# Widening 64-row products of a graph network kernel to all 128 rows of TensorE with zeros

## The reference

```python
h = jnp.maximum(_layernorm(x, axis=-1), 0.0)        # [3125, 64], before each layer
# layer 1 (relations): for each of 8 relations r
h_r = x @ W[r]                                       # [N, 64] @ [64, 64]
s, d = h_r @ att_src[r], h_r @ att_dst[r]
out = x @ W_self + b_self + sum over r of the attention sums of h_r
# layer 2 (edge network): [x[start], x[end]] @ We1   = x @ We1[:64] and x @ We1[64:]
# layer 3 (GATv2)
xl, xr = x @ W_l + b_l, x @ W_r + b_r                # [N, 64] @ [64, 256], twice
```

## Time and profile before

| | |
|---|---|
| median of 3 runs | 5458.55 us (5458.1 to 5464.73) |
| the profiled execution | 5454.14 us, span 5452.2 us |
| busy share: PE, DVE, ACT, POOL | 53%, 74%, 14%, 66% |
| mean granted TensorE clock | 0.776 of full speed |
| chain that ended last | POOL 49%, issue 20%, PE 13%, DVE 10%, DMA 5% |

### The profile page before, as it was taken

The page is one execution under the profiler, slowest core; times in us unless marked ns, Lnnn a source line. Parts: engine busy times, 40 slices in busy tenths (PEclk is TensorE's granted clock), DMA queues, the critical chain, the costliest instruction groups (busy, mean ns, idle before and its releaser), DMA issues.

```text
span 5452.2 us, 62157 instructions
## 1 busy us (share of the span) xinstructions
PE 2898.0 (53%) x10645; PEld 1413.7 (26%) x10645; DVE 4041.3 (74%) x10615; ACT 778.0 (14%) x1976; POOL 3590.8 (66%) x3635
## 2 busy tenths in 40 slices
PE   5743374136677000006455555554787777828983
PEld 4522121013566000003122222221333323303332
DVE  8857995245999997655677777745788888888982
ACT  0000021010000014540122222220000000003330
POOL 0677777771777887765777777743777777715651
PEclk9999976565999555555787767765889999869995
DMA  9121364211544338871565555524999999918980
GB/s 382 55 85 37 114 244 153 79 67 66 191 161 163 118 122 316 300 271 49 177 179 181 181 179 181 180 83 150 307 308 310 312 310 306 313 49 313 334 296 13
DMA packets 454207, 1040.84 MB, mean 191 GB/s; under 512 B 129077, under 2 KB 247325, under 8 KB 423796
## 3 DMA queue, kind: packets, MB, share of 16 engines
q1 hardware_dynamic: 162930, 580.42, 29.2%
q0 software_dynamic: 131968, 217.09, 14.5%
q10 hardware_dynamic: 159234, 242.47, 12.7%
HBM read 560.07 MB, written 477.20 MB: 190 GB/s over the span
## 4 chain that ended last, share of the span: by engine, by line
POOL 49%; issue 20%; PE 13%; DVE 10%; DMA 5%; another core or an unknown queue 2%; DVEq 1%; POOLq 0%; ACT 0%; ACTq 0%; SPq 0%
POOL arena L646 32%; POOL weights L679 15%; PE psum L1248 3%; PE psum L1197 3%; PE psum L1198 3%; DMA arena<-tab,ring 3%; PE psum L1032 2%; DVE arena L2029 1%; DVE arena L1770 1%; DVE arena L1534 1%; POOL agg L666 1%; POOL arena L666 1%; DVE arena L1957 1%; DVE arena L1672 0%
## 5 line engine op out<-in xcount | busy, mean ns | idle before, releaser
L646 POOL DMA_INDIRECT arena<-tab,ring x2352 | 2338.1, 994 | 717.5 <-issue 702.8
L1197 PE MATMUL psum<-arena,ident 128*128 128x512 f32 x1176 | 779.5, 751 | 732.4 <-DMA arena<-tab,ring 569.3
L679 POOL DMA_INDIRECT weights<-arena x784 | 829.5, 1058 | 382.9 <-issue 238.7
L1534 DVE SCALAR_TENSOR_TENSOR arena<-arena,ns 128x64 f32<-128x64 f32 (+2 forms) x2351 | 868.6, 369 | 186.6 <-ACT arena L864 49.1
L1198 PE MATMUL psum<-arena,ident 128*128 128x512 f32 x1176 | 724.2, 702 | 0.0
L1197 PEld LDWEIGHTS psum<-arena,ident 128*128 128x128 f32 x1176 | 260.7, 237 | 1155.6 <-issue 627.9
L744 POOL TENSOR_TENSOR arena<-arena,score 128x256 f32<-128x256 f32 x294 | 232.5, 816 | 281.0 <-DMA arena<-spill 126.8
L1248 PE MATMUL psum<-arena,ident 128*128 128x512 f32 x784 | 362.5, 608 | 68.9 <-DVE arena L2029 68.6
L1957 DVE SCALAR_TENSOR_TENSOR arena<-psum,rowb 128x1024 f32<-128x1024 f32 x196 | 239.0, 1219 | 194.8 <-PE psum L1198 194.6
L1198 PEld LDWEIGHTS psum<-arena,ident 128*128 128x128 f32 x1176 | 270.2, 230 | 377.0 <-issue 377.0
L1120 PE MATMUL psum<-arena 64*128 64x400 f32 x512 | 158.6, 705 | 359.9 <-DVE arena L1581 352.2
(11 more groups left out here) (366 smaller groups left out, 4490.0 us busy)
## 6 DMA issues: line engine op xcount, KB each, us to landing
put<-zero SPq DMA_DIRECT2D x98, 1040.0 KB
arena<-put SPq DMA_DIRECT2D x98, 1040.0 KB, 7.7
spill<-arena ACTq DMA_DIRECT2D x98, 1024.0 KB, 5.4
arena<-spill SPq DMA_DIRECT2D x98, 1024.0 KB
state<-arena ACTq DMA_DIRECT2D x147, 512.0 KB, 3.4
weights<-zero SPq DMA_DIRECT2D x1, 51200.0 KB, 130.9
arena<-weights SPq DMA_DIRECT2D x32, 1600.0 KB, 7.8
put<-zero SPq DMA_DIRECT2D x14, 3584.0 KB
```

The lines of the kernel that those rows point to most:

```text
L646: pool.indirect_dma_start(out=rows[:, h, k, :], out_offset=None, in_=table[:, :], in_offset=bass.IndirectOffsetOnAxis(ap=ring[:, h, word + ...
L679: pool.indirect_dma_start(out=weights0[:, :], out_offset=bass.IndirectOffsetOnAxis(ap=words0[:, g, k:k + 1], axis=0), in_=words0f[:, g, K ...
L1197: pe.matmul(place, lhsT=ident[:, :], rhs=rows_of[0][:, s, columns, 0:width], start=True, stop=False)
L1534: beats.add(dve.scalar_tensor_tensor(out=rows[:, s, k, :], in0=before, scalar=mark(ns, g, k), in1=rows[:, s, k, :], op0=ALU.mult, op1=ALU. ...
```

## The change

`hT` and four weight matrices as well as `wa` get all 128 partitions. The kernel goes on writing only partitions 0 to 63 of them. POOL sets partitions 64 to 127 to zero once at the start. `mix` multiplies with the full 128 rows, for the stationary operand and the streaming one, so that the upper half adds products of zeros. PE waits once, ahead of phase 1, until the zeros are there. Everything else, and the products of layer 0 (phase 0), of the edge network's second half (phase 4) and of the feed-forward (phase 6), keeps its 64 rows.

```diff
-        hT = sb("hT", [D, NB, P])
+        hT_full = sb("hT", [P, NB, P])
+        hT = hT_full[0:D, :, :]
...
-        w0_sb, wself_sb, wrel_sb = sb("w0_sb", [D, 2, D]), sb("wself_sb", [D, D]), sb("wrel_sb", [D, R, D])
-        we1_sb = sb("we1_sb", [D, 2, HID])
+        w0_sb, wself_full, wrel_full = sb("w0_sb", [D, 2, D]), sb("wself_sb", [P, D]), sb("wrel_sb", [P, R, D])
+        we1_full, wlr_full, wa_full = sb("we1_sb", [P, 2, HID]), sb("wlr_sb", [P, 2, HD]), sb("wa", [P, 2, R])
+        wself_sb, wrel_sb, we1_sb, wlr_sb, wa = (full[0:D] for full in (wself_full, wrel_full, we1_full, wlr_full, wa_full))
...
+            for full in (hT_full, wrel_full, we1_full, wlr_full, wa_full):
+                tally.done(pool.memset(full[D:P, :, :], 0.0), consts)
+            tally.done(pool.memset(wself_full[D:P, :], 0.0), consts)
...
-                    return pe.matmul(bank(0, 6)[:, at + j * width:at + (j + 1) * width], lhsT=hT[:, j, :], rhs=rhs, start=True, stop=True)
+                    return pe.matmul(bank(0, 6)[:, at + j * width:at + (j + 1) * width], lhsT=hT_full[:, j, :], rhs=rhs, start=True, stop=True)
...
-            wrel_all = wrel_sb[:, :, :].rearrange("d r f -> d (r f)")
-            products(1, lambda b: mix(1, b, wrel_all, wa[:, :, :].rearrange("d a r -> d (a r)")))
+            wrel_all = wrel_full[:, :, :].rearrange("d r f -> d (r f)")
+            pe.wait_ge(consts, 16)
+            products(1, lambda b: mix(1, b, wrel_all, wa_full[:, :, :].rearrange("d a r -> d (a r)")))
...
-            products(2, lambda b: mix(2, b, wrel_all, wself_sb[:, :]))
+            products(2, lambda b: mix(2, b, wrel_all, wself_full[:, :]))
...
-            products(3, lambda b: mix(3, b, we1_sb[:, :, :].rearrange("d a f -> d (a f)"), cut=False))
+            products(3, lambda b: mix(3, b, we1_full[:, :, :].rearrange("d a f -> d (a f)"), cut=False))
...
-            products(5, lambda b: mix(5, b, wlr_sb[:, :, :].rearrange("d a f -> d (a f)")))
+            products(5, lambda b: mix(5, b, wlr_full[:, :, :].rearrange("d a f -> d (a f)")))
```

More of the change, by code:

```diff
@@ L214, in gnn_program @@
         sc = sb("sc", [P, 16])
-        w0_sb, wself_sb, wrel_sb = sb("w0_sb", [D, 2, D]), sb("wself_sb", [D, D]), sb("wrel_sb", [D, R, D])
-        we1_sb = sb("we1_sb", [D, 2, HID])
+        w0_sb, wself_full, wrel_full = sb("w0_sb", [D, 2, D]), sb("wself_sb", [P, D]), sb("wrel_sb", [P, R, D])
+        we1_full, wlr_full, wa_full = sb("we1_sb", [P, 2, HID]), sb("wlr_sb", [P, 2, HD]), sb("wa", [P, 2, R])
+        wself_sb, wrel_sb, we1_sb, wlr_sb, wa = (full[0:D] for full in (wself_full, wrel_full, we1_full, wlr_full, wa_full))
         wn1m_sb, wn1h_sb, wn2_sb = sb("wn1m_sb", [2 * D, HID]), sb("wn1h_sb", [D, HID]), sb("wn2_sb", [HID, D])
-        wlr_sb = sb("wlr_sb", [D, 2, HD])
         wf1_sb, wf2_sb = sb("wf1_sb", [D, FF]), sb("wf2_sb", [P, 2, D])
@@ L221, in gnn_program @@
         colb = sb("colb", [P, 4])
-        wa = sb("wa", [D, 2, R])
         lowest = sb("lowest", [P, D])
```

## The result

The changed kernel takes 5438.19 us (median of 6 runs, 5432.43 to 5440.63), the kernel before 5460.53 us (6 runs, 5458.1 to 5464.73). The ratio is 0.9957, with a 95% interval from 0.9944 to 0.9969: 22 us less, 17 to 31. The forecast was 5437 us.

The account below looks back on a forecast made before the run. PE's low-clock products were taken to bound phase 1 and parts of phases 3 and 5. Gains 18.7 + 0 + 2.5 + 0.4 = 21.6 us took 5454.14 to 5432.5, plus 4.4 for the median: 5437 us, range 5430 to 5450.

Parts of the forecast that it names:

- What holds the clock down: Phases 1, 2, 3 and 5: products using 64 of 128 rows keep PE's clock at 0.50; the high clock halves full-height products.
- Phase 1, 18.7 us: Four batches gain 4.2 us each as the period falls from 13.1 to 8.9, the first 1.9; bounds 12.8 and 20.5.
- The ring through the write of `tb1`: Phase 1: the single buffer makes each batch's copies wait for the previous table write, limiting the period to 8.9 us.
- The slack of 1.8 us in each batch: Phase 1: PE needs 7.1 of 8.9 us, so 3.6 us of each batch could run at the low clock.
- the rival that has the clock rise late: Phase 1: each batch spends 6.1 us at the low clock, PE needs 10.2; total gain near 14 us, chance 0.17.
- Phase 2, nothing: Phase 2: no gain, since POOL's collection releases DVE's sum over `agg` and doesn't wait for PE.
- Phase 3, 2.5 us: Phase 3: faster products let POOL's 25 scatters go back to back; gain 2.5 us, bounds 0 and 3.1.
- Phase 5, 0.4 us: Phase 5: only the first part of the first batch counts; gain 0.4 us, at most 0.8, possibly nothing.
- The zeros: Start of kernel: six POOL memsets, 3.1 us together, fit in POOL's idle time and cost nothing.
- The clock did not stay down: Rival for the changed phases: something other than rows holds the clock, products keep their times, 5458 to 5459 us; chance 0.12.
- Loads of 128 rows cost nothing: Rival judged here: full-height loads in phases 1, 3 and 5 are no longer hidden, +19 us, 5478 us; chance 0.03.
- every product counts in full: Rival: products of phases 1, 2, 3 and 5 all shorten the kernel, by 75 us to 5384 us; chance 0.03.

Follow-up runs that it names:

- e5: Changed kernel with ones instead of zeros in the weights' partitions 64 to 127: 7877.88 us in one run, on a chip where the kernel before took 7922.74.
- e4: Kernel with all products back at 64 rows, plus 12 unread 128-row products on PE ahead of phase 1: 5462.45 us in one run.
- e3: Changed kernel with phases 1 and 3 multiplying over 96 rows, phases 2 and 5 over 80: 5444.0 us in one run.
- e11: All products over 64 rows as before the change, plus four unread 128-row products ahead of phase 6: 5437.24 us, ratio 0.9963 to the kernel before.
- e1: Changed kernel with phases 2, 3 and 5 back at 64 rows, only phase 1 over 128: 5445.14 us, ratio 0.9966 to the kernel before.
- e7: Changed kernel with a second buffer for phase 1's table rows: 7897.74 us, ratio 0.9967 to the kernel before on a chip where that took 7922.74.
- e6: Changed kernel with phases 4 and 6 over 128 rows too: 7884.74 us, ratio 0.9953 to the kernel before on a chip where that took 7922.74.
- e2: Changed kernel with phase 1 back at 64 rows, phases 2, 3 and 5 over 128: 5460.38 us, ratio 0.9993 to the kernel before.
- e8: Changed kernel plus unread 128-row products ahead of phases 1, 3, 5 and 6: 7875.97 us, ratio 0.9945 to the kernel before on its chip.

## Why the prediction was right, step by step

**What holds the clock down.** The step "what sets the products of phases 1, 2, 3 and 5 apart is that they use 64 of 128 rows" holds. All four phases left 0.50; e5 takes the values in one operand away as a reason, e4 the pauses and the cold start. It was too simple in one point: e3 shows that the same 96 rows do for phase 1 and not for phase 3, and e11 shows that a mix of 64-row and 128-row work which stays at 0.50 from a low start keeps 1.00 from a high one. On row count the Trainium skill's page "TensorE: Matmul & The Clock Gate", in Part 1 and in its table of "Why this matters for your kernels", gives no reason for a gain. The runs settle it against that reading: 97% busy with 64 rows stays at 0.50 (e4, 10.71 of 11.00 us), and the same work over 128 rows comes back to the high clock.

**Phase 1, 18.7 us.** 19.2 in the profile, 19.4 in e1. The period was put at 8.9 us and is 8.79. The ring through the write of `tb1` was named as the next bound, and e7 shows it: a second buffer takes the period to 7.09 us, the 7.1 worked out for PE alone. The first batch was worth 2.4 us (8.66 in place of 11.03 in the chain), forecast 1.9. The slack of 1.8 us in each batch was needed: the clock falls in the third and the last batch (6.23 and 5.97 us for the wide products) and the period doesn't show it. It is not always enough. In e6 one batch took the 10.2 us of the rival that has the clock rise late, and phase 1 gave 17.1 us. So the mechanism and its size were right, but a forecast of 5437 us for a measured 5438.19 is nearer than the mechanism can promise, and that closeness is luck. The sum takes the falls of the clock as hidden in every batch; only its range allows for one that isn't.

**Phase 2, nothing.** From the first collection of `betas` to the first of `agg` POOL takes 40.5 us (2442.45 to 2482.90) where it took 40.6, and DVE's wait for `agg` has grown from 0.47 us to

```profile
2515.68 1.82 DVE L1814 TENSOR_TENSOR xn<-xn,agg 128x1600 f32<-128x1600 f32 x1 [4.10 <-DMA agg<-state,eidx]
```

**Phase 3, 2.5 us.** The 25 scatters of the earlier trace rows now reach from 2538.96 to 2569.31, 30.35 us in place of 32.94, with 0.30 us between all of them. That is 2.6 us, the whole of what could shrink.

```profile
2538.96 1.00 POOL L639 DMA_INDIRECT put<-arena,zidx  x1 [24.90 <-DVE arena L1828]
...
2569.31 0.96 POOL L639 DMA_INDIRECT put<-arena,zidx  x1 [0.30 <-issue]
```

**Phase 5, 0.4 us.** DVE's first wait was 6.00 us and is 5.10, the third batch starts 15.0 us after the second as before:

```profile
3680.39 0.96 DVE L1943 TENSOR_TENSOR arena<-psum,rowb 128x768 f32<-128x768 f32 x1 [5.10 <-PE psum L1036]
...
3694.98 0.96 DVE L1943 TENSOR_TENSOR arena<-psum,rowb 128x768 f32<-128x768 f32 x1 [3.16 <-DMA tab<-arena]
...
3709.98 0.96 DVE L1943 TENSOR_TENSOR arena<-psum,rowb 128x768 f32<-128x768 f32 x1 [3.12 <-DMA tab<-arena]
```

0.9 us, a little over the bound of 0.8: the clock rose in the first six matmuls (4.59 us in the chain, 5.50 before). In e2 the same wait is 5.56 us, so this term moves too.

**The zeros.** Six memsets from 4.65 to 7.16 us on POOL, in its idle time of the earlier trace rows. Nothing, as forecast.

**The rivals.** The clock did not stay down, nor did it rise late in every batch (10.2 us for PE, against a period of 8.79; e6 shows it in one of its batches). Loads of 128 rows cost nothing: ten wide matmuls take 4.54 us with them. That every product counts in full is refuted by e2, where phases 2, 3 and 5, to which that rival gave 53.5 of its 75 us, gave 4.2 us.

## What to carry to other kernels

Read the granted clock of each stretch before costing products: a stretch of busy PE at 0.50 is worth half its matmul time, but only as far as the next ring allows, so work out that ring (here one buffer and its write) first. Where operands fill only 64 rows, zeros to 128 rows cost nothing here and can raise the clock. Where the work is mixed, a few unused 128-row products in a pause just before the phase may be enough. Such filler has to wait for what the phase waits for, or it will stand in its way, and the clock it earns can be lost again in the first batch. Read a gain of a few us from the phase, since the whole time moves by more than that from run to run.

## What the runs showed that was not expected

- The clock keeps its state. Phase 6 with the same products runs at 0.50 from a low start (50.2 us) and at 1.00 after four filler products (29.5 us in e8, 30.1 in e11). I had expected it to fall back, as it did in phase 1 of e4. In both runs it was lost some 27 us after the first wf1 products, as the phase ended, so that a longer phase would keep it isn't shown.
- 96 rows got 0.85 in phase 1 and 0.50 in phase 3; 80 rows got 0.50 in phases 2 and 5 (e3).
- At the start of the trace the granted clock can mislead: between 396 and 431 us it reads 1.00, while five transposes there take 1.25 us, their time at the low clock (0.71 at the high one). The duration of a known shape is the better witness.
- One chip took 45% longer for the kernel before (7922.74 us), yet phase 1 took there what it takes elsewhere (56.6 us in e5, 56.7 in the changed kernel, from the first transposes to the first gather).
